# The products inside a chunk, in two column halves of TensorE's array

## What is computed

```python
xdt = (x * dt[..., None]).reshape(b, c, CHUNK, h, p)
Lmat = jnp.exp(segsum(Adt))                      # zero where the source token is later
Y_diag = jnp.einsum('bcln,bcsn,bhcls,bcshp->bclhp', Cr, Br, Lmat, xdt)
Y_off = jnp.einsum('bcln,bchpn,bhcl->bclhp', Cr, states_prev, jnp.exp(Acs))
```

## Time and profile before

| | |
|---|---|
| runs | 3191.86, 3184.94, 3186.76 us |
| median | 3186.76 us |
| span of the profiled execution, first to last instruction | 3185.9 us |
| TensorE (PE), products | 3112.3 us busy, 98% of the span |
| TensorE, weight loads (PEld) | 2722.1 us, 85% |
| VectorE (DVE) | 2394.2 us, 75% |
| GpSimd (POOL) | 2031.2 us, 64% |
| ScalarE (ACT) | 1935.2 us, 61% |
| line 1575, products | 2048 records, 246.1 us busy |

### The profile page before, as it was taken

How to read it: one execution, slowest core, us unless ns; L and a number is a source line. 1 busy time by engine, 2 the same in 40 slices (tenths; PEclk the granted TensorE clock), 3 DMA queues, 4 the chain that set the end, 5 groups by cost and what they waited for, 6 DMA issues and landing times.

```text
span 3185.9 us, 62383 instructions
## 1 busy us (share of the span) xinstructions
PE 3112.3 (98%) x19648; PEld 2722.1 (85%) x19648; DVE 2394.2 (75%) x5104; ACT 1935.2 (61%) x4149; POOL 2031.2 (64%) x2311
## 2 busy tenths in 40 slices
PE   5899999999999999999999999999999999999997
PEld 4688888888888888888888888888888888888886
DVE  5877877777777777777777777778777777777763
ACT  5565666665666556666566666656656656665562
POOL 2477666677666676656676666776666776666764
PEclk7899999999999999999999999999999999999999
DMA  3123222222222222222122222222222222222222
GB/s 123 41 68 87 73 73 67 66 66 85 73 64 64 71 73 76 80 66 58 64 86 76 76 60 66 66 86 73 73 66 66 66 86 73 64 67 69 73 74 48
DMA packets 143433, 227.33 MB, mean 71 GB/s; under 512 B 18976, under 2 KB 88352, under 8 KB 143392
## 3 DMA queue, kind: packets, MB, share of 16 engines
q1 hardware_dynamic: 126496, 210.06, 20.1%
q0 software_dynamic: 16896, 16.78, 4.0%
HBM read 174.87 MB, written 35.13 MB: 66 GB/s over the span
## 4 chain that ended last, share of the span: by engine, by line
PE 95%; DVE 0%; POOL 0%; ACT 0%; issue 0%; ACTq 0%; DVEq 0%; POOLq 0%
PE fpb L1443 34%; PE apb L1443 20%; PE acc L1629 17%; PE apb L1575 7%; PE apb L1452 4%; PE ppb L1443 3%; PE apb L1560 3%; PE apb L1567 2%; PE ppb L1462 2%; PE apb L1547 1%; PE fpb L1492 1%; PE fpb L1462 1%; PE fpb L1494 1%; PE fpb L1608 0%; PE apb L1520 0%; PE apb L1519 0%
## 5 line engine op out<-in xcount | busy, mean ns | idle before, releaser
L652 POOL TENSOR_TENSOR hidL<-hid,hidH 128x512 fp32r<-128x512 f32 x384 | 544.9, 1419 | 234.8 <-ACT hidH L914 226.8
L1130 DVE SCALAR_TENSOR_TENSOR xc<-apb,cw,xc 128x511 f32<-128x511 f32 (+2 forms) x576 | 427.8, 747 | 63.9 <-ACT xc L827 35.9
L1629 PE MATMUL acc<-WDH,hidH 128*128 128x256 f32 x1536 | 456.7, 297 | 4.4 <-POOLq L654 4.4
L914 ACT CAST hidH<-hid 128x512 fp32r<-128x512 f32 x384 | 236.2, 615 | 341.9 <-POOL hid L647 283.6
L1629 PE MATMUL acc<-WDH,hidL 128*128 128x256 f32 x1536 | 431.4, 281 | 0.0
L1629 PE MATMUL acc<-WDL,hidH 128*128 128x256 f32 x1536 | 430.9, 281 | 0.0
L647 POOL TENSOR_TENSOR hid<-hid,cb 128x512 f32<-128x512 f32 x256 | 347.5, 1358 | 73.2 <-DVEq L1251 42.1
L1249 DVE TENSOR_TENSOR hid<-hid,fpb 128x512 f32<-128x512 f32 x384 | 261.1, 680 | 135.6 <-PE fpb L1443 132.3
L1443 PE MATMUL fpb<-fTh,UH 128*128 128x512 f32 x768 | 335.7, 437 | 0.0
L845 ACT ACTIVATE seg<-seg,acs 128x128 f32<-128x128 f32 x1024 | 313.6, 389 | 11.5 <-ACT cb L895 5.7
L1443 PE MATMUL fpb<-fTh,GH 128*128 128x512 f32 x768 | 318.6, 415 | 0.0
(11 more groups left out here) (195 smaller groups left out, 8669.6 us busy)
## 6 DMA issues: line engine op xcount, KB each, us to landing
seg<-acs_row SPq DMA_DIRECT2D x128, 512.0 KB, 4.2
cb<-c_row SPq DMA_DIRECT2D x512, 128.0 KB, 2.9
xsP<-in_x SPq DMA_DIRECT2D x32, 512.0 KB, 3.6
xc<-qrot SPq DMA_DIRECT2D x32, 512.0 KB, 3.4
xc<-in_x SPq DMA_DIRECT2D x32, 512.0 KB, 4.3
out<-xc SPq DMA_DIRECT2D x32, 512.0 KB, 3.0
out<-xn POOLq DMA_DIRECT2D x32, 512.0 KB, 6.0
ZL_loaded<-in_wzx_t SPq DMA_DIRECT2D x2, 512.0 KB, 4.4
```

The costliest lines, as they stand in the source:

```text
L652: own.do(G.tensor_tensor(hidL[:, j % 2, :], hid[:, j % 2, :], hidH[:, j % 2, :].bitcast(fp32), ALU.subtract))
L914: A.copy(hidH[:, j % 2, :], hid[:, j % 2, :]).then_inc(sem["hidden_high"], 1)
L1130: ins = V.scalar_tensor_tensor(xc[:, b, s:], src[:, 0:T - s], cw[:, b, TAPS - 1 - s:TAPS - s], xc[:, b, s:], ALU.mult, ALU.add)
L1629: ins = nc.tensor.matmul(dst, l[:, w, tk], r[:, j, :], start=j == 0 and t % 2 == 0 and n == 0, stop=j == HB - 1 and n == 2, skip_group_che ...
```

## The change

Each head's stationary block of 128 columns (the tokens that are written) is cut in two of 64 columns. The first half's product writes PSUM partitions 0 to 63, the second half's 64 to 127, both with the same moving operand of 64 columns. Each is one column half of the array. There are twice as many products and loads on this line; arithmetic, bank, waits and the signal after the last product stay.

```diff
@@ -1572,7 +1572,10 @@
                 pe.wait_ge(sem["m_ready"], c + 1)
                 for h in range(HS):
                     hs = slice(h * PD, (h + 1) * PD)
-                    ins = nc.tensor.matmul(b[:, hs], seg[:, c % 2, h, :], xdt[:, c % 2, hs], start=True, stop=True)
+                    for r in range(0, P, P // 2):
+                        rows_ = slice(r, r + P // 2)
+                        ins = nc.tensor.matmul(b[rows_, hs], seg[:, c % 2, h, rows_], xdt[:, c % 2, hs],
+                                               start=True, stop=True)
                 fill(f"yd{c}", ins)
```

## The result

The changed kernel takes 3127.13 us (median of four runs, 3126.12 to 3135.33), beside 3186.56 us for the kernel before: a ratio of 0.9815, with a 95% interval of 0.98 to 0.9829. In a second group of five runs the ratio was 0.9821 (0.9808 to 0.9835). It is 59 us faster. The forecast of 3232 us was wrong in sign: a loss of 46 us was expected. The first rival, with both halves loading side by side, had put it at 3121 us.

A forecast was written before the change was run, and what follows sets the result against it. TensorE was taken as the bound; each diagonal going from 1.73 to 1.95 us, plus exits, made 1.43 us a sequence, times 32 is 46 us on 3186.8: 3232 us. The range to hold 8 in 10 was 3117 to 3252.

The forecast's parts named there:

- The bound: Whole kernel: TensorE holds 95% of the chain of waits, so a nanosecond added to its loop stream lengthens the kernel.
- What limits line 1575: Diagonal's products before the change: loads 0.112 us apart are the bound, over streams of 0.054 us.
- Load slots: Diagonal's 64-column loads: 0.056 us a pair in alternate halves, so 31 pairs take 1.74 us where fifteen took 1.68.
- Entering and leaving: Diagonal's ends: first pair 0.21 us in place of 0.05; exit 0.15 us each, 0.10 before transposes.
- The lower bound with no switch: Diagonal: serial loads without switch cost, 1.79 us, kernel 3194 us; chance 0.07 together with a gain the switches eat.
- The upper bound: Diagonal: instructions no faster than one in 0.03 us make a pair 0.06, the diagonal 2.07, the kernel 3247 us.
- Side by side: Diagonal: halves load and stream in parallel, 0.028 us a pair, 1.08 a diagonal, kernel 3121 us; chance 0.31 with weaker form.
- Its weaker form: Diagonal: starts in program order, 0.042 us a pair, 1.51 a diagonal, kernel 3176 us; within the shared chance of 0.31.
- Loads and streams stop overlapping: Diagonal: a load waits for the other half's product, 0.11 us a pair, 3.62 a diagonal, kernel 3447 us; chance 0.08.
- the forecast's own 3194 to 3250: Whole kernel: range in us for the forecast case, serial load slots with switch costs; chance 0.54.

The follow-up runs named there:

- after_again: The changed kernel unchanged, run and profiled a second time in another group beside the kernel before: 3130.21 us, ratio 0.9821.
- the run with two heads: Changed kernel with both products of heads 0 and 1 in half 0, then in half 1, and so on: 3135.02 us, ratio 0.9822.

## Why the prediction was wrong

**The bound.** Right. TensorE was full before and is full after, and what it saved came out almost whole: 1.90 us a sequence of 2.02 by the pieces.

**What limits line 1575.** Right, and it pointed at the result: loads of 0.112 over streams of 0.054, which two parallel loads lift.

**Load slots.** This step failed. I took 0.056 us a pair in alternate halves because line 1520's two loads followed each other by a slot in proportion to their columns. They did so in one and the same part of the array. Measured: 0.028 where the halves alternate, 0.058 where pairs follow each other in one half. So the slot of 0.056 for 64 columns was right, and what failed is that the halves share it: they don't. The row that I called nearest was near in form and far in the one thing that mattered, and the text had said so and given both ends. The sign of the whole forecast hung on that one choice: 31 x 0.028 = 0.87 us a diagonal, 111 us a run.

The Trainium skill's page "TensorEngine Tiling (Array Packing)", section "Key Properties", says that tiles load and multiply in parallel; the runs agree, at 1.08 against 1.83 us for the order alone. I had set beside my 0.056 what the Trainium skill's page "TensorE: Matmul & The Clock Gate", section "Weight-path perf modes", says on fp32 and a fast load of the full array. It does not carry over to two tiles.

**Entering and leaving.** Entry 0.21 for the first pair: 1.08 - 31 x 0.028 = 0.21, or 0.18 if the steady 0.029 is taken; right. Exit 0.15 expected, and from diagonal to diagonal the four cost 0.14, 0.16, 0.19 and 0.15 in `after_again`. The one before transposes, for which I took 0.10, was the dearest: what I took off for their shorter load wasn't there. That is 0.09 us a sequence, 2.9 us in all. The lower bound with no switch was wrong to hang on line 1608: its transposes with 16 columns show no cost of a switch, and line 1520's product does.

**The upper bound.** A product every 0.06 us if instructions came only every 0.03: wrong by far. A diagonal of 64 pairs holds 128 instructions in 1.10 us.

**The rivals.** "Side by side" had the mechanism and the diagonal to the digit, 1.08 us, and 66 us of gain where 59 came; of the missing 7 us the exits are 2.9 and waits on GpSimd 1.6 in the profiled run (four turns of 0.4), and the rest isn't told apart from the scatter of the medians. Its weaker form, with starts in program order, falls by the 1.08 us, where it had 1.51, and again by the run with two heads. "Loads and streams stop overlapping" falls: 3.6 us was foretold for a diagonal. The Trainium skill's page "TensorE: Matmul & The Clock Gate", section "The mechanism", has loads overlap products only where row groups differ, in its list of what overlaps; a sentence above that list also lets a load go ahead into the array's background weights. Here both halves share all rows, and in each half a slot of 0.058 us holds a load and a stream of 0.054 at once. The measurement decides against the list, for column halves as for the full array, and agrees with the other sentence.

**The chances.** 0.31 for the case that came true was low. The range of 3117 to 3252 held the result only because it was stretched to take that rival in; the forecast's own 3194 to 3250 did not.

## What to carry to other kernels

A short product that waits on its weight load (loads further apart than its stream is long) can be cut in two column halves of the stationary tile, taken in turns. Here that brought 0.058 us for what took 0.112. What counts is that neighbours in the order go to different halves, or that no more than three pairs of one half stand in the way. Each entry into the half width and exit from it costs about 0.15 us of a full TensorE, so by these figures, as an estimate, it pays from about six full-width pairs in a row on (0.3 / 0.054). Look then for narrow products elsewhere that pay the same switch unasked, and try padding them to the full width. And count the loop body: pairs that halve the time of a stage double its instructions, and between 1543 and 1671 TensorE instructions this loop began to stall at every turn.

## What the runs showed that was not expected

- A pair for the other half starts past three waiting pairs of the first, in runs of four (1.13 against 1.08 us) and at the seam between runs of sixteen (1.83), and no further.
- Pairs of 32 columns in quarters start every 0.014 us on average, against 0.028 for halves; 128 loads and products pass in 1.10 us.
- A TensorE loop body of 1543 instructions stays where it is; one of 1671 is fetched again each turn (278 instruction packets against 24), and with its stops the granted clock falls to 0.50 for 3.4 to 6.8 us a turn. The kernel is then 3.2% over the one before.
- Padding a stationary tile from 32 to 128 columns saved 0.24 us each time.
- Saving 2 us of TensorE a turn was enough for GpSimd to hold a product up by 0.4 us in some turns.
